# A two-layer graph network on one core: fewer adjacency loads in the prologue, x in four transfers, row loads first in a tile

## The reference

```python
mask = (adj > 0).astype(x.dtype)
deg = jnp.sum(mask, axis=1, keepdims=True)
agg = mask @ x / jnp.maximum(deg, 1.0)          # x here is h = relu(layernorm(x))
combined = jnp.concatenate([x @ W_self + b_self, agg @ W_nb + b_nb], axis=-1)
out = relu(combined @ W_comb + b_comb)          # layer 0; x1 = x + out
...
Wh = (H @ W).reshape(n, N_HEADS, D_K)           # layer 1, H = relu(layernorm(x1)), 4 heads of 64
e = leaky_relu(sl[:, :, None] + sr.T[None, :, :], 0.2), masked by A + eye
out = elu(softmax(e, axis=2) @ Wh)              # result = x1 + out
```

## Time and profile before

| what | us |
|---|---|
| median of 3 runs (lowest, highest) | 913.51 (909.61, 919.68) |
| profiled execution | 917.63 |
| its span | 915.8 |
| TensorE busy in the span | 816.3 (89%) |
| VectorE busy | 696.4 (76%) |
| ScalarE busy | 563.1 (61%) |

### The profile page before, as it was taken

The page is one execution under the profiler, slowest core; times in us unless marked ns, Lnnn a source line. Parts: engine busy times, 40 slices in busy tenths (PEclk is TensorE's granted clock), DMA queues, the critical chain, the costliest instruction groups (busy, mean ns, idle before and its releaser), DMA issues.

```text
span 915.8 us, 26041 instructions
## 1 busy us (share of the span) xinstructions
PE 816.3 (89%) x10789; PEld 736.5 (80%) x10789; DVE 696.4 (76%) x1339; ACT 563.1 (61%) x839; POOL 132.2 (14%) x253
## 2 busy tenths in 40 slices
PE   5564569799999999986999999999999999999995
PEld 4222237688888888875999999999999999999995
DVE  3524376567767777747889899988999889998884
ACT  3423230122222222228899999999998999989992
POOL 0000023444444444430000000000000000000000
PEclk9867788899999999997999999999999999999998
DMA  8676749999798999944004101141011311111011
GB/s 186 181 185 177 178 138 285 300 301 286 221 296 214 268 278 251 285 95 107 21 5 92 46 11 36 46 92 46 0 46 47 72 31 34 46 47 33 13 23 34
DMA packets 90268, 115.67 MB, mean 126 GB/s; under 512 B 61769, under 2 KB 63625, under 8 KB 90217
## 3 DMA queue, kind: packets, MB, share of 16 engines
q1 hardware_dynamic: 71256, 67.33, 29.2%
q10 hardware_dynamic: 9024, 26.88, 11.1%
q0 software_dynamic: 9936, 20.86, 7.9%
HBM read 98.17 MB, written 16.85 MB: 126 GB/s over the span
## 4 chain that ended last, share of the span: by engine, by line
PE 36%; DMA 18%; DVE 17%; ACT 11%; SPq 8%; issue 5%; POOL 3%; DVEq 0%; POOLq 0%
DMA rows<-in_x 10%; ACT stage L763 7%; PE ps_x L634 7%; PE ps_t L634 7%; PE ps_a L634 7%; SPq L334 7%; DMA mask<-in_x 4%; PE ps_w L634 4%; PE ps_h L634 4%; DVE stage L1057 3%; PE ps_t L582 3%; PE ps_t L584 3%; DMA own_scratch<-mask 2%; POOL rows L474 2%; DVE bits L951 2%
## 5 line engine op out<-in xcount | busy, mean ns | idle before, releaser
L582 PE MATMUL ps_t<-g,mask 128*128 128x257 f16 x1024 | 233.8, 277 | 2.9 <-DVE mask L958 2.9
L584 PE MATMUL ps_t<-g,mask 128*128 128x256 f16 x1024 | 233.7, 276 | 0.0
L763 ACT ACTIVATE stage<-rows,sr 128x1024 int8<-128x1024 f32 x192 | 204.2, 1171 | 5.7 <-PE ps_w L634 5.7
L763 ACT ACTIVATE stage<-bits,sr 128x1024 int8<-128x1024 f32 x192 | 204.4, 1170 | 2.4 <-PE ps_w L634 2.4
L1057 DVE SCALAR_TENSOR_TENSOR stage<-stage,mask 128x1024 int32<-128x1024 int32 x128 | 156.6, 1223 | 21.8 <-ACT stage L763 21.1
L634 PE MATMUL ps_x<-g,stage 128*128 128x130 f16 x2048 | 158.8, 220 | 9.7 <-DVE stage L1068 4.7
L634 PE MATMUL ps_t<-g,stage 128*128 128x130 f16 x2048 | 158.4, 219 | 0.0
L634 PE MATMUL ps_a<-g,stage 128*128 128x130 f16 x2048 | 158.4, 219 | 0.0
L634 PEld LDWEIGHTS ps_x<-g,stage 128*128 128x128 fp8e4 x2048 | 127.5, 97 | 11.8 <-issue 11.7
L634 PEld LDWEIGHTS ps_t<-g,stage 128*128 128x128 fp8e4 x2048 | 127.3, 97 | 0.2
L634 PEld LDWEIGHTS ps_a<-g,stage 128*128 128x128 fp8e4 x2048 | 127.3, 97 | 0.2
(11 more groups left out here) (131 smaller groups left out, 925.6 us busy)
## 6 DMA issues: line engine op xcount, KB each, us to landing
mask<-in_adj SPq DMA_DIRECT2D x98, 256.0 KB, 8.3
stage<-in_adj SPq DMA_DIRECT2D x58, 256.0 KB, 8.2
mask<-in_adj ACTq DMA_DIRECT2D x54, 256.0 KB, 10.0
stage<-in_adj ACTq DMA_DIRECT2D x46, 256.0 KB, 9.7
own_scratch<-mask POOLq DMA_DIRECT2D x16, 256.0 KB, 7.7
rows<-own_scratch POOLq DMA_DIRECT2D x32, 128.0 KB, 7.3
rows<-in_x POOLq DMA_DIRECT2D x128, 32.0 KB, 8.3
x_scratch<-late POOLq DMA_DIRECT2D x32, 128.0 KB, 7.1
```

The costliest lines, as they stand in the source:

```text
L582: nc.tensor.matmul(ps_t32[e][:, 0:D + 1], at, g[:, 2 * kk + b, D:2 * D + 1], start=kk + b == 0, stop=kk == NK - 1 and b == 1, skip_group_c ...
L584: last = nc.tensor.matmul(ps_t32[e][:, 0:D], at, g[:, 2 * kk + b, 0:D], start=False, stop=kk == NK - 1 and b == 1, skip_group_check=True)
L763: nc.scalar.activation(sign_bytes(sgn, k, b), srow[gr % 2].rearrange("p (r n) -> p r n", n=2 * P), ACT.Sign, bias=sr[:, 2 * k + b, H + gr ...
```

## The change

Six edits. `x_rows` issues every pair by four transfers. In the prologue SyncE issues one quarter for each three pairs (k = 4, 7, 10, 13: quarters 1 to 4), so quarters 5 and up come behind the x of pair 15. BOTH is 9: quarters 9 to 13 too are shared with ScalarE's queue. In the tile loop GpSimd loads `row(t + 2)` first, as soon as x1 of tile t is there. The column of scores is stored from GpSimd's queue in tile 9 (`t == NJ + 1`) and no longer by SyncE. VectorE does `to_bits` of quarter 63 behind `low_h1T` of its tile and not ahead of it.

```diff
@@ x_rows @@
-            if k < 2:
-                for a in range(UN):
-                    eng.dma_start(xin[k % XR][a * UP:(a + 1) * UP, :], x_v[a, k]).then_inc(x_in[k % XR], 16)
-            else:
-                eng.dma_start(xin[k % XR], x_v[:, k]).then_inc(x_in[k % XR], 16)
+            for a in range(UN):
+                eng.dma_start(xin[k % XR][a * UP:(a + 1) * UP, :], x_v[a, k]).then_inc(x_in[k % XR], 16)
@@ SyncE @@
                 x_rows(sp, k)
-                adj_rows(sp, k - XR + 1, range(UN))
-            for n in range(NK - XR + 1, 2 * NT):
+                if k % 3 == 1:
+                    adj_rows(sp, k // 3, range(UN))
+            for n in range(NK // 3, 2 * NT):
                 adj_rows(sp, n, range(UN if n < BOTH else UN // 2))
-            sp.wait_ge(sr_ready, NJ)
-            with nc.allow_non_contiguous_dma("s is turned from a column into a row"):
-                for e in range(2):
-                    sp.dma_start(s0_d.rearrange("o (j p e) -> e p (o j)", p=P, e=2)[e],
-                                 sr[:, 0:NJ, 0:1].rearrange("p (j e) o -> p e (j o)", e=2)[:, e]).then_inc(late_out, 16)
-
-            sp.wait_ge(late_out, 32)
+            sp.wait_ge(s0_out, 32)
             sp.wait_ge(turned, NT * 2)
@@ GpSimd @@
             for t in range(NT):
+                if t + 2 < NT:
+                    pool.wait_ge(x1_ready, t + 1)
+                    row(t + 2)
                 if t:
                     store_wh(t - 1)
                 store_x1(t)
-                if t + 2 < NT:
-                    row(t + 2)
+                if t == NJ + 1:
+
+                    pool.wait_ge(sr_ready, NJ)
+                    with nc.allow_non_contiguous_dma("s is turned from a column into a row"):
+                        for e in range(2):
+                            pool.dma_start(s0_d.rearrange("o (j p e) -> e p (o j)", p=P, e=2)[e],
+                                           sr[:, 0:NJ, 0:1].rearrange("p (j e) o -> p e (j o)", e=2)[:, e]
+                                           ).then_inc(s0_out, 16)
@@ VectorE, tile loop @@
                 if more:
                     turn(n)
+                if n + 2 < 2 * NT:
                     to_bits(n + 1)
                 low_h1T(t, t % 2)
+                if n + 2 == 2 * NT:
+                    to_bits(n + 1)
                 if more:
                     turn(n + 1)
@@ -1281,7 +1283,7 @@
-BOTH = 14
+BOTH = 9
```

More of the change, by code:

```diff
@@ L246, in build @@
         late_out = sem("late_out")
+        s0_out = sem("s0_out")
         rmax_ready = sem("rmax_ready")
@@ L299, in x_rows @@
         def x_rows(eng, k):
-            if k < 2:
-                for a in range(UN):
-                    eng.dma_start(xin[k % XR][a * UP:(a + 1) * UP, :], x_v[a, k]).then_inc(x_in[k % XR], 16)
-            else:
-                eng.dma_start(xin[k % XR], x_v[:, k]).then_inc(x_in[k % XR], 16)
-        def x_landed(eng, k):
-            eng.wait_ge(x_in[k % XR], k // XR * 16 + (16 * UN if k % XR < 2 else 16))
+            for a in range(UN):
+                eng.dma_start(xin[k % XR][a * UP:(a + 1) * UP, :], x_v[a, k]).then_inc(x_in[k % XR], 16)
         def slot_free(eng, n):
@@ L389, in _ @@
             sp.dma_start(wh_d[NT - 1], wh[:, 1, :]).then_inc(late_out, 16)
-            sp.wait_ge(late_out, 48)
+            sp.wait_ge(late_out, 16)
             for e in range(2):
@@ L856, in variances @@
             def variances(k):
-                x_landed(dve, k)
+                dve.wait_ge(x_in[k % XR], (k // XR + 1) * 16 * UN)
                 for e in range(2):
```

## The result

The changed kernel takes 860.63 us in the median of four runs (858.59 to 865.33), the kernel before 914.48 us beside it (909.61 to 919.68): a ratio of 0.942, interval 0.935 to 0.948, or 54 us gained. The profiled execution took 865.33 us, its span 863.3. "Stage start" is TensorE's first aggregation product and "end" its last one.

| | before | after | forecast |
|---|---|---|---|
| stage start, us | 136.0 | 84.8 | 94 |
| aggregation, us | 279.4 | 278.5 | 272 |
| what follows, us | 500.4 | 500.0 | 500.4 |
| span, us | 915.8 | 863.3 | 867 |

A forecast was written before the change was run, and what follows sets the result against it. Prologue bound: each pair's x on 4 of 16 DMA engines. Gains of 42 us there and 7 in the aggregation off 917.63 gave 868.6, or 865 for the median, the profiled execution being 4.1 above it; range 842 to 893.

The forecast's parts named there:

- the new wait of `to_bits` for raw quarters: Aggregation: a sign of being right, that VectorE's `to_bits` would now wait for quarters to arrive; no size given.
- 4 of 16 engines: Prologue: a pair's x, one transfer over four blocks, lands on four DMA engines, 144 KB each, 7.7 us a pair.
- number of transfers counts: Prologue, rival: each SyncE issue costs 1.98 us whatever its size, aggregation starts 18 us later, 925 us; chance 0.04.
- the estimate of 5.9 us a pair: Prologue: transfers served one after another at the skill page's times; the aggregation would start 23 us later than forecast.
- I take 4.1: Prologue: period of a pair in us, between bounds 3.6 and 6.0, near the loop between VectorE and TensorE.
- 3.8 for pairs at the half clock: Prologue: 3.8 us added to the stage start for two first pairs with TensorE at the half clock.
- DMA takes over as the bound of this stage: Aggregation: moving quarters, rows and stores sets its length, 272 against 279.4 us, so only 7 us gained.
- the 253 us for the quarters: Aggregation: time to move quarters, rows and stores until quarter 63 has landed, at a chosen 280 GB/s.
- Most of the 29.6 us of waits go: Aggregation: issuing row loads 3.5 to 4 us sooner removes most of VectorE's wait for a tile's rows.
- 0 to 4 us once: End of the aggregation's quarters: bounds for the gain from storing the column of scores early; taken at nothing.
- Only the first, behind the stores of the last own rows, stays: Aggregation start: of VectorE's row waits only the first remains, behind own-row stores that take 15.8 us to land.
- the aggregation gives much of it back: Aggregation, rival: less stock, DMA at 246 GB/s, stage 307 us, 28 more than before, 899 us total; chance 0.12.

The follow-up runs named there:

- rows_last: Changed kernel with a tile's row loads put behind its two stores again, as before; 869.15 us, ratio 0.951.
- s0_back: Changed kernel with the column of scores stored by SyncE behind its last quarter again; 859.69 us, ratio 0.941.
- s0_pieces: Changed kernel with the column of scores stored by GpSimd in eight pieces of 128 elements, in tiles 2 to 9; 857.64 us, ratio 0.941.
- start_fix: Changed kernel with rows of tiles 0 and 1 loaded after the ninth pair's store, the wait for the last own-row stores moved to tile 28; 851.77 us, ratio 0.934.
- split_only: Kernel before with only every pair's x in four transfers, still a quarter per pair; 871.95 us, ratio 0.957.
- split_thin: Kernel before with only the two prologue edits, x in four transfers and one quarter per three pairs; 870.73 us, ratio 0.956.
- combined: start_fix plus the column of scores stored in eight pieces; 853.22 us, ratio 0.935.
- x_two_blocks: Changed kernel with a pair's x in two transfers, each a view of two blocks of 32 rows; 920.64 us, ratio 1.008.
- thin_only: Kernel before with only one quarter per three pairs in the prologue, x still in one transfer; 892.66 us, ratio 0.979.
- stores_between: combined with GpSimd issuing the Wh and x1 stores between a tile's own-row load and its four x loads; 853.85 us, ratio 0.935.

## Why the prediction was right, and where it was not

The time was forecast at 865.0 and is 860.63; the sign and the range held. Two of its terms were off, one to each side: the prologue gave 51 us where 42 were forecast, the aggregation 1 to 3 where 7 were. That the sum came within 5 us is in part luck. Of the signs named for being right one failed, the new wait of `to_bits` for raw quarters; none of those for being wrong came.

**The cause of the prologue's length: shown.** "4 of 16 engines" carried x: the split alone takes 38 us off the start, relieving the four engines alone 33, and x on two engines puts it 62 us behind the kernel after. But the row that the prediction read this from does not show it. In the kernel before, from 120 to 125, the share of 0.23 is by queue (q0 is GpSimd's, with an own-row store):

```profile
q0 software_dynamic: 88, 0.29, 15.0%
q1 hardware_dynamic: 75, 0.16, 8.2%
```

So two thirds of it were not x, and that it came out near 4/16 was luck; the 23.9% of SyncE's queue from 116 to 118 is the row that bears the reading. The rival "number of transfers counts" is refuted: SyncE's timeline of the kernel after has five issues of x in 2.99 us at 59.77, 0.6 each, where 1.7 each were needed. The Trainium skill (DMA: Bandwidth & Descriptors, "Measured (HBM→SBUF, 128 partitions, SWDGE, issued from GpSimd)") wants transfers of 1 MiB or more; the estimate of 5.9 us a pair from that page did not come (3.46), and here four of 64 KB beat one of 256 KB. That is no test of its rule for transfers spread alike: no run here has a pair's x as one transfer over all engines.

**The step that was mis-sized there:** "I take 4.1", and 3.8 for pairs at the half clock. The period is 3.46 from pair 5 to 13, with neither `ownA` nor SyncE's queue in the way, and TensorE was at its full level from pair 2 on. Pair 2 to pair 15 took 48.0 us (24.8 to 72.9 on VectorE), where 13 x 4.1 and the 3.8 make 57.1; that is the whole miss. The start came at 84.8, not 94, near the lower bound given: 51 us gained, not 42. The prediction did not have VectorE's own work among its limits, and it is the one that holds: the loop and TensorE's work were put at 3.6, and VectorE, which never waits for another engine from 36.6 to 67.7, takes 3.46.

**The aggregation: the bound was wrong.** "DMA takes over as the bound of this stage" failed. No wait for a quarter shows in the kernel after, and DMA moved 306 GB/s from 85 to 110 and 316 from 110 to 170. The 271 and 301 GB/s of rows 1 were therefore no limit of the engines, though the 253 us for the quarters was chosen from between them. From 170 to 364 it moved 251 GB/s at a share of 0.92 and still no quarter was waited for: the quarters were ahead, and the rate was that of the demand. The prediction used this same argument against its rival and not against itself. The stage was still held up, 278.5 and 276.2 in its two profiles, not 272: by the first tiles' rows and by the stores of x1, as below.

**The rows' wait went, but not its time.** 29.6 us became 5.2, as said. "Most of the 29.6 us of waits go" left out what was put behind the five row loads: the x1 store is issued behind them, 4.8 us after the first (188.03 to 192.86) and takes 9.0 us to land instead of 7.1. It stood for 20.0 us of VectorE's waits, and TensorE's stall stayed (17.7 and 14.1 against 14.7). That the move is still worth having shows in rows_last (869.15).

**The s row: "0 to 4 us once", taken at nothing.** The wait for the last quarter that it takes away was 4.55 us and comes back as 3.56 in s0_back; in tile 9 the store causes waits of 7.94 and 8.52. By the medians the two cancel (s0_back 859.69), and s0_pieces, with neither, is at best 3 to 4 us faster. So nothing was near enough for the time, though not for the reason given.

**The first tiles.** "Only the first, behind the stores of the last own rows, stays" was said of the rows' wait; together with the wait for the last own-row stores ahead of tile 2's rows it is the largest single loss found, 10 us of the median (start_fix).

**The fallback.** That the thinner prologue takes from the aggregation ("the aggregation gives much of it back", 0.12) is real in size, 9.0 us from split_only to split_thin. Its mechanism, DMA at 246 GB/s, is not: what grows there is the wait for rows.

**What stays open:** why the pieces, worth at best 3 to 4 us by themselves, are worth nothing on top of start_fix. ScalarE's idle time behind its own issues grew (20.8 us in start_fix, 28.3 in combined, by the waits), which may be part of it; no run took that away. The move of `to_bits(63)` has no run of its own. That it was `to_bits` that slows GpSimd's issues is read from their overlap alone (the pair of lines in the last section).

## What to carry to other kernels

Here a load whose DRAM view had an outer dimension of 4 ran on four DMA engines, and of 2 on two; the sign is a DMA share near that fraction while one consumer waits (read by queue, since another queue's transfers can make up the same share), and the cure is to issue it in slices of partitions, even small ones. A rate read from a kernel that waits elsewhere is its demand, so no bound should be worked out from it without a wait that ends on that transfer. When loads go ahead of stores on one queue, ask who waits for the stores. A stage length from one profile compares two kernels only as well as two single executions do: look where the profiled execution stands among the others. And place a store of single elements where no waited-for transfer runs beside it, or cut it up.

## What the runs showed of the hardware

A store of 1024 elements of 4 bytes went with a stretch of about 5 us in which the DMA engines showed shares of 0.92 to 0.99 and 64 to 91 GB/s (s0_back, the kernel after), and a neighbouring 128 KB store took 17.31 us; in eight pieces no slump shows (299 and 304 GB/s). Mixed loads and stores ran at 316 GB/s over 60 us.

A load whose view confines it to few engines also held the queue that issued it: SyncE's six issues of x from 33.28 in x_two_blocks took 19.18 us, three from 19.57 in thin_only 13.80, where twelve from 37.31 in the kernel after took 7.80.

GpSimd's issue of four x loads takes 1.98 us where no `to_bits` runs (in the kernel after at 114.49; in rows_last, where they are issued later in a tile, 519 ns each in the mean) and 3.72 us beside VectorE's `to_bits`. VectorE in the kernel after, during GpSimd's issue from 188.58 to 192.30:

```profile
188.48 1.23 DVE L950 TENSOR_SCALAR bits<-mask 128x2048 uint8<-128x2048 int32 x1
...
190.52 1.19 DVE L950 TENSOR_SCALAR bits<-stage 128x2048 uint8<-128x2048 int32 x1
```

The two operations last 2.42 us together, a little more than the 1.74 us that the issue is longer. The Trainium skill (SBUF — State Buffer, "SBUF: two separate sides") describes such a lock between VectorE's faster modes and GpSimd's writing of descriptors; the doubled issue agrees with it, and the kernel gained nothing measurable when the issues were moved away (stores_between).
